# Order of the first two images' work in a log-polar convolution: differences of x first, weights of the second half last, another warm-up

## What is computed

```python
xp = log_pooling(x)                                   # fixed 9x9 masks, 4*3 averages per pixel
out = conv(xp, w_conv1, strides=(4, 3))               # 256 x 12 -> 256 channels
out = out + conv(x, w_center) + b_center              # 1x1
mean, var = out.mean(axis=(0, 2, 3)), out.var(axis=(0, 2, 3))
out = (out - mean) * rsqrt(var + 1e-5) * gamma + beta
return relu(out + x)
```

## Time and profile before

| | before |
|---|---|
| median of 3 runs | 1656.84 us |
| the profiled execution | 1657.47 us |
| its span, first to last instruction | 1655.8 us |
| TensorE busy | 1483.6 us (90%) |
| VectorE busy | 1419.4 us (86%) |
| ScalarE busy | 641.7 us (39%) |
| mean granted TensorE clock | 0.949 |

### The profile page before, as it was taken

How to read it: one execution, slowest core, us unless ns; L and a number is a source line. 1 busy time by engine, 2 the same in 40 slices (tenths; PEclk the granted TensorE clock), 3 DMA queues, 4 the chain that set the end, 5 groups by cost and what they waited for, 6 DMA issues and landing times.

```text
span 1655.8 us, 22787 instructions
## 1 busy us (share of the span) xinstructions
PE 1483.6 (90%) x8468; PEld 1481.7 (89%) x8468; DVE 1419.4 (86%) x1327; ACT 641.7 (39%) x689; POOL 112.5 (7%) x146
## 2 busy tenths in 40 slices
PE   6999999999999999999999999999999999992000
PEld 6999999999999999999999999999999999992000
DVE  7999898988988889898898888988989988886323
ACT  3234434334334343433433434343343333434423
POOL 1000000000000000000000000000000000000000
PEclk8999999999999999999999999999999999997555
DMA  6455554555545555455545555545554555579999
GB/s 198 105 130 144 134 133 123 124 143 123 118 123 131 143 134 134 125 121 143 132 111 121 131 142 134 135 126 120 141 130 115 120 132 141 134 244 420 425 425 382
DMA packets 65479, 268.75 MB, mean 162 GB/s; under 512 B 7616, under 2 KB 7616, under 8 KB 65472
## 3 DMA queue, kind: packets, MB, share of 16 engines
q1 hardware_dynamic: 42176, 173.38, 31.1%
q0 software_dynamic: 18432, 69.61, 24.3%
q10 hardware_dynamic: 4864, 25.69, 3.7%
HBM read 218.07 MB, written 50.58 MB: 162 GB/s over the span
## 4 chain that ended last, share of the span: by engine, by line
PE 86%; SPq 5%; DMA 4%; DVE 3%; ACT 1%; issue 1%; ACTq 0%; DVEq 0%; POOLq 0%
PE acc L664 29%; PE acc L665 29%; PE acc L666 29%; SPq L311 3%; DMA phase<-x 2%; SPq L308 2%; DMA row<-x_wide 1%; DMA out<-phase 1%; DVE pooled L448 1%; ACT phase L440 0%; DVE pooled_split L449 0%; DVE inner_split L449 0%; ACT m_copy L396 0%; DVE y_stage L448 0%; DVE row3v L448 0%
## 5 line engine op out<-in xcount | busy, mean ns | idle before, releaser
L380 ACT ACTIVATE pooled_split<-pooled 128x1456 fp32r<-128x1456 f32 x192 | 273.4, 1425 | 611.0 <-DVE pooled L448 611.0
L449 DVE TENSOR_TENSOR pooled_split<-pooled,pooled_split 128x1456 fp32r<-128x1456 f32 x192 | 315.2, 1669 | 0.3 <-ACT pooled_split L380 0.3
L664 PE MATMUL acc<-pooled_split,w_first 128*128 128x364 f32 x768 | 253.3, 330 | 3.9 <-DVE pooled_split L449 3.9
L665 PE MATMUL acc<-pooled_split,w_first 128*128 128x364 f32 x768 | 253.8, 330 | 0.0
L666 PE MATMUL acc<-pooled_split,w_first 128*128 128x364 f32 x768 | 252.9, 329 | 0.0
L665 PE MATMUL acc<-pooled_split,w_outer 128*128 128x364 f32 x768 | 252.2, 328 | 0.0
L664 PE MATMUL acc<-pooled_split,w_outer 128*128 128x364 f32 x768 | 252.2, 328 | 0.0
L666 PE MATMUL acc<-pooled_split,w_outer 128*128 128x364 f32 x768 | 251.8, 328 | 0.0
L664 PE MATMUL acc<-inner_split,w_first 128*128 128x406 f32 (+1 forms) x640 | 223.5, 349 | 13.5 <-DVE inner_split L449 10.1
L666 PE MATMUL acc<-inner_split,w_first 128*128 128x406 f32 (+1 forms) x640 | 223.1, 349 | 0.0
L665 PE MATMUL acc<-inner_split,w_first 128*128 128x406 f32 (+1 forms) x640 | 223.0, 348 | 0.0
(11 more groups left out here) (81 smaller groups left out, 2139.4 us busy)
## 6 DMA issues: line engine op xcount, KB each, us to landing
row<-x_wide SPq DMA_DIRECT2D x64, 558.0 KB, 3.7
row<-x_wide POOLq DMA_DIRECT2D x64, 558.0 KB, 7.3
ends<-x_wide SPq DMA_DIRECT2D x64, 504.0 KB, 3.9
ends<-x_wide POOLq DMA_DIRECT2D x64, 504.0 KB, 5.8
x_pad<-x SPq DMA_DIRECT2D x64, 392.0 KB, 3.1
y_dram<-y_stage SPq DMA_DIRECT2D x31, 784.0 KB, 8.7
phase<-y_dram SPq DMA_DIRECT2D x30, 784.0 KB, 28.6
phase<-x SPq DMA_DIRECT2D x30, 784.0 KB, 30.3
```

Of the source, the lines that this page charges most:

```text
L380: nc.scalar.activation(view(pooled_split, 2 * j * PAIR, (1, PAIR)), view(pooled, (PAIRS * c + j) % 2 * PAIR, (1, PAIR)), ACT.Copy)\
L449: sub = lambda out_, a, b: nc.vector.tensor_tensor(out_, a, b, ALU.subtract)
L664: nc.tensor.matmul(place, hi_w, hi_in, start=start, stop=False)
L665: nc.tensor.matmul(place, lo_w, hi_in, start=False, stop=False)
```

## The change

Five things change, all in image 0 and image 1:

1. VectorE computes the first half's differences of x first, and calls `transform_weights(c)` right behind them, in both halves of image 0 (before: the first half's ahead of all, the second half's in the middle of the first half).
2. VectorE makes the lo parts of the inner weights after the lo part of `inner`, and those of the outer weights after the pooled sums (before: one step earlier each).
3. ScalarE copies `inner` first, then all seven groups of the first half's weights, then the three pooled sums, and only then all seven groups of the second half's weights.
4. In image 1 VectorE takes y of image 0 before `box4` instead of after the pooled sums.
5. The warm-up is 16 matmuls of 392 columns and 62 of 202 columns (406 // 2 - 1), in place of 20 of 392.

```diff
-        WARM_UP = 20
+        WARM_UP, WARM_UP_SHORT = 16, 62
+        SHORT = WINDOW // 2 - 1
...
                     if first and c == 0:
-                        split_weights(0, range(FIRST_OUTER_GROUP - 1, len(GROUPS)))
-                        split_weights(1, range(len(GROUPS)))
+                        split_weights(0, range(len(GROUPS)))
                         act.wait_ge(warmed_up, 1)
                     for j in range(PAIRS):
                         split_pooled(s, c, j)
+                    if first and c == 0:
+                        split_weights(1, range(len(GROUPS)))
...
             act.wait_ge(zeroed, ZEROED)
-            split_weights(0, range(INNER_GROUPS))
             image_steps(0, first=True)
...
                         view(d03, 1, (U * TALL + 1, 2), (TALL, U), (1, H))).then_inc(v_ready, 1)
                     if first:
-                        lo_of_weights(c, range(INNER_GROUPS))
+                        transform_weights(c)
...
                         view(inner_split, 0, (1, SD)).bitcast(F32)).then_inc(inner_lo_ready, 1)
+                    if first:
+                        lo_of_weights(c, range(INNER_GROUPS))
...
-                    if first:
-                        lo_of_weights(c, range(FIRST_OUTER_GROUP - 1, len(GROUPS)))
-                        if c == 0:
-                            transform_weights(1)
+                    if second and c == 0:
+                        take_y(image - 1)
...
+                    if first:
+                        lo_of_weights(c, range(FIRST_OUTER_GROUP - 1, len(GROUPS)))
                     lo_of_pooled(s, c, 0)
-                    if c == 0 and not first:
+                    if c == 0 and not first and not second:
                         take_y(image - 1)
...
-            transform_weights(0)
             image_steps(0, first=True)
...
-            for k in range(WARM_UP):
-                warm = nc.tensor.matmul(view(acc, 7 * BANK, (1, HALF)), zeros[:, 0:P], zeros,
+            for k in range(WARM_UP + WARM_UP_SHORT):
+                n = HALF if k < WARM_UP else SHORT
+                warm = nc.tensor.matmul(view(acc, 7 * BANK, (1, n)), zeros[:, 0:P], view(pooled_split, 0, (1, n)),
                                         start=True, stop=True)
```

## The result

The changed kernel takes 1662.95 us (median of 6 runs, 1661.77 to 1664.25) against 1656.66 us for the kernel before on the same chip (6 runs, 1656.39 to 1657.08). The ratio is 1.0038, with a 95% interval of 1.0028 to 1.0048: 6.3 us slower. The forecast was 1661.5 us, slower by 4.7, with a range of 1657.5 to 1664.0. By the means, 1662.8 against 1656.7 us, it is 6.1 slower.

The account below looks back on a forecast made before the run. TensorE sets the pace in the long middle, so only the first 130 us count, where VectorE's steps are the chain. 3.1 (V/D of image 2) + 1.6 (clock) = 4.7 on 1656.84 gives 1661.5 us, range 1657.5 to 1664.0.

Parts of the forecast that it names:

- Differences of x first: Image 0, first half: VectorE arrives earlier but waits longer at row3 for the unchanged accumulating DMA; gain 0 us.
- The standstill: Image 0, second half: VectorE waits for ScalarE's copy of inner behind seven weight copies, 4.1 + 1.6 = 5.7 us.
- VectorE's lateness: From the lo of inner in image 0's second half on, VectorE is 5.4 us later than before.
- The new waits of TensorE: Image 0's second half, image 1's second half and y in image 2: over 6, 1.1 and 2.8 us.
- The clock after the last wait: Behind the 2.8 us wait in image 2, the low clock costs 1.6 us, bounds 0 and 2.8.
- Rival A: Image 2: same wait, but the clock stays up; +3.1 us, 1659.9 us; chance 0.25.
- The warm-up: Start of TensorE: 16 long and 62 short matmuls end at 12 us, or 24 if dearer; price and gain 0 us.
- The sum: Whole kernel: +3.1 and +1.6 make +4.7 us, so 1661.5 us, 0.28% slower.
- V/D of image 2 later: Image 2: TensorE's V/D block waits for y and begins at 133.15 instead of 130.04, 3.1 us later.
- B: Image 2's V/D block or image 1's 1.1 us pause: clock lost more dearly, +5.9 to +7 us; chance 0.15.
- C: Image 0, second half: VectorE's standstill doesn't reach TensorE; 0.8 to 3.6 us faster; chance 0.10.
- D: Start and image 0: the moved steps do nothing measurable, everything within +-2 us; chance 0.05 on its own.

Follow-up runs that it names:

- e8_m_after_row2: The changed kernel with TensorE's first real block held until the accumulating DMA of row2 has landed: 1662.77 us, ratio 1.0033 to the kernel before.
- e1_inner_first: The changed kernel with ScalarE copying inner ahead of the second half's weights in image 0's second half: 1657.54 us, ratio 1.0003 to the kernel before.
- e3_y_early_only: The kernel before with only y of image 0 taken ahead of box4 in image 1: 1657.11 us, ratio 1.0001.
- r0_after_again: The changed kernel measured once more, no edit: 1663.13 us, ratio 1.0037 to the kernel before.
- e4: The changed kernel with the old warm-up of 20 matmuls: 1662.08 us, ratio 1.0031 to the kernel before.
- e2_warmup_only: The kernel before with the new warm-up alone: 1656.71 us, ratio 1.0000.
- e9_all_three_new_warmup: The changed kernel, new warm-up kept, with inner copied ahead of the second half's weights and y early in image 2 too: 1653.72 us, ratio 0.9982 to the kernel before.

## Why the prediction was right, and where its sizes were off

*Differences of x first: 0 us.* Right for the order: VectorE began at 4.08 us and waited 5.65 us for the DMA. What the step missed is that `row3` comes 0.94 us later (20.28 for 19.34): the accumulating DMA takes 9.69 us instead of 9.00 beside the earlier, faster M block, and starts 0.27 us later (10.58 for 10.31) behind a load of 7.67 us. In e8_m_after_row2 the DMA is short again. I had written that nothing in the change touches that transfer; that is the term which failed, 0.7 us in size here. The other 0.27 us are the load, which varies in the same way without the change.

*The standstill: 5.7 us.* Right: 5.67, and gone in e1_inner_first with the loss. VectorE's lateness of 5.4 us was 6.2 at y of image 1 (132.12 for 125.90), which is 5.3 for the order and 0.9 for the later `row3`.

*The new waits of TensorE.* Expected near 51, 100.7 and 133.15 us; seen at 51.87, 101.56 and 134.03, each 0.9 us later for that same reason. Their lengths, over 6, 1.1 and 2.8 us, were 6.18, 1.09 and 2.56.

*The clock after the last wait: 1.6 us, between 0 and 2.8.* Measured by the V/D block of image 2, which takes 4.31 us with no pause ahead of it: 4.41 us with the clock up (the changed kernel's first profile, e3_y_early_only), 5.94 or 5.95 with the clock lost (r0_after_again, e1, e4 and e8), so 0.1 or 1.6 us for a pause of 2.55 to 2.58 us. The size was right; that it comes in some executions only was not foreseen. The result's own six runs lost it, by their spans, in two. Rival A (the clock stays up) was thus what the first profiled execution did and most of these runs, the forecast what four of the six profiles with this pause did. The advice of the Trainium skill ("TensorE: Matmul & The Clock Gate", section "Why this matters for your kernels") to leave no longer pauses than about 3 us, read as saying that shorter ones are safe, does not hold in these traces: four of six such pauses lost it, and so did the one of 1.96 us in e1_inner_first.

*The warm-up: 0 us.* Right on the chain (e2_warmup_only, 1656.71 against 1656.65). It ended at 13.5 us, not 12 (12.7 to 14.2 in the other profiles), still ahead of what mattered. The sum lacked the time outside the span: in the six runs of the result it is 1.92 to 3.13 us, 2.5 in the mean, where 1.68 is usual with the old warm-up. It is less in other runs of the long warm-up (last section; median 1.69 in r0_after_again), so these 0.8 us are a mark of those six runs and not a fixed price.

*The sum.* +4.7 us was forecast, +6.1 measured by the means. In the forecast's terms:

| term | forecast | measured |
|---|---|---|
| V/D of image 2 later | 3.1 | 4.0 |
| clock behind the pause | 1.6 | 0.5 |
| the execution compared with | 0 | 0.8 |
| time outside the span | 0 | 0.8 |
| sum | 4.7 | 6.1 |

The 4.0 is read from the profile. The 0.5 is what the six spans (mean 1660.3 us) have above the profiled one with the clock up, 1659.8. The 0.8 in the third line is 1655.8, the span of the execution that the sum was made against, less 1655.0, an estimate for the runs of before in the result: their mean, 1656.7, less the usual 1.68 outside the span. Adding +4.7 to the median of before hid it. At least a part of it is the dear clock loss of image 1 (7.01 us for the V/D block, 5.94 in e2_warmup_only); which of the executions of before lost how much was not profiled, so this part is argued from two profiles, not shown.

So the waits were right, and the total came within 1.6 us in part by luck: the clock term was three times too large for these runs, and three others were too small. The measured median, 1662.95, lies just above the forecast's own range (1660.2 to 1662.7), in the band that was given to B.

*The rivals.* C, that VectorE's standstill doesn't reach TensorE, is excluded by e1_inner_first. A had the clock right for most of the six runs, but its total of 1659.9 is 3 us short, for the terms of the table. B, a dearer clock, did not appear, though the total fell into its band: the pause of 1.1 us ahead of image 1's second half kept the clock in the first profile (V/D there follows M after 108.37 - 101.56 = 6.8 us). D, everything within 2 us, is out at +6.3.

## What to carry to other kernels

When a producer and a consumer each work through a fixed list, look at what stands ahead of the one item that the other is about to need: 4 us of weight copies that had been free in the idle time of ScalarE cost VectorE 5.7 us when they were moved ahead of one copy of 1.5 us. A start that is moved up is worth nothing if the next step waits for a transfer; look for the first wait whose instant doesn't depend on the order. And a late engine shows itself at every later meeting point, so an edit that removes one wait (y early in image 1) must be followed on to the next (y in image 2); here two such edits together were worth 3.4 us and the first alone nothing that could be measured. Last, a forecast that is made against one profiled execution inherits what was particular in it; here that was 0.8 us.

## What the runs showed of the hardware that was not expected

- The same pause of TensorE, 2.56 us at the same place, was followed by the 1.2 GHz level in one execution and by 2.4 GHz in another, with 5.95 and 4.41 us for the same 24 matmuls. A pause of 1.96 us (e1_inner_first) was followed by a granted clock of 0.70 between 48 and 52 us, one of 2.18 (e9_all_three_new_warmup, at 23.08) by 0.57 between 24 and 28; none of the pauses of 1.1 to 1.7 us was.
- With 78 warm-up matmuls instead of 20 the time outside the span (execution less span) grew. In all kernels with the old warm-up it was 1.62 to 1.74 us in every run that shows it; in those with the new one it was 1.61 to 3.14: in 25 of 55 runs 1.90 to 2.00, in 19 as with the old one (in e9_all_three_new_warmup eight of eleven between 1.82 and 1.99). The cause was not tried.
- The accumulating DMA of 558 KB at the start took 8.9 us with TensorE's real blocks held back, 8.9 to 9.2 in the six other profiles with a late or slow M block, and 9.6 to 9.8 us in four of the five with a fast M block beside it (9.25 in the fifth).
